# Four edits at the end of the recurrence of a one-layer decoder: row buffer slots, first attention rows, query weights, waits for stores

## The reference, cut to what matters

```python
# x (4, 2048, 512), ctx (4, 77, 512), all float32
x = x + recurrence(layernorm(x), ...)               # diagonal plus low rank state space, over time
x = x + cross_attention(layernorm(x), ctx, Wq, Wk, Wv, Wo)   # 16 heads of 32, 77 keys
x = x + ffn(layernorm(x), ...)                      # expand to 2048, butterflies, gelu, contract
...
def step(z, u_t):                                   # x.reshape(T, B, 8, 64): "T" is the batch axis
    y = A * z + u_t
    z_new = jnp.einsum('hk,bpk->bph', V, y)
    return (z_new, z_new)
```

## Time and profile before

| | us |
|---|---|
| median of 3 runs | 2243.32 (2242.6 to 2244.34) |
| profiled execution, its own time | 2245.92 |
| span of its trace | 2244.1 |
| PE busy | 2208.0 (98%) |
| DVE busy | 1710.0 (76%) |
| ACT busy | 1230.7 (55%) |
| POOL busy | 471.8 (21%) |
| mean granted TensorE clock | 0.992 |

### The profile page before, as it was taken

How to read it: one execution, slowest core, us unless ns; L and a number is a source line. 1 busy time by engine, 2 the same in 40 slices (tenths; PEclk the granted TensorE clock), 3 DMA queues, 4 the chain that set the end, 5 groups by cost and what they waited for, 6 DMA issues and landing times.

```text
span 2244.1 us, 41303 instructions
## 1 busy us (share of the span) xinstructions
PE 2208.0 (98%) x15960; PEld 1938.0 (86%) x15960; DVE 1710.0 (76%) x2868; ACT 1230.7 (55%) x2749; POOL 471.8 (21%) x578
## 2 busy tenths in 40 slices
PE   8999889999999999999999999999999999999999
PEld 7788678888888888789989989989989989889899
DVE  6775588888988888857858858758669578579467
ACT  3666567766666766735536446446346356355343
POOL 3530222232322322200200300300300300201203
PEclk8999899999999999999999999999999999999999
DMA  9999613323323322476785786686676776766765
GB/s 321 338 356 307 211 60 131 119 84 123 126 86 114 123 92 90 168 244 180 217 270 172 223 269 184 214 267 208 198 259 209 226 229 208 250 207 209 227 189 194
DMA packets 202092, 443.36 MB, mean 198 GB/s; under 512 B 32442, under 2 KB 70586, under 8 KB 200362
## 3 DMA queue, kind: packets, MB, share of 16 engines
q1 hardware_dynamic: 201898, 440.72, 60.8%
HBM read 341.66 MB, written 99.01 MB: 196 GB/s over the span
## 4 chain that ended last, share of the span: by engine, by line
PE 88%; DVE 5%; DMA 3%; ACT 2%; issue 1%; SPq 0%; POOL 0%; DVEq 0%; ACTq 0%; POOLq 0%
PE ps L456 71%; PE ps L2027 5%; PE ps L1995 4%; PE ps L2006 3%; DMA x_scratch<-xa 2%; PE ps L1911 1%; PE ps L1954 1%; PE ps L1842 1%; ACT es L1106 1%; DVE st L1299 1%; DMA x<-x_scratch 1%; DVE ptl L1336 1%; PE ps L1884 0%; PE ps L1871 0%; PE ps L1807 0%
## 5 line engine op out<-in xcount | busy, mean ns | idle before, releaser
L456 PE MATMUL ps<-ring,gh 128*128 128x256 f32 x3584 | 652.8, 284 | 0.1
L456 PEld LDWEIGHTS ps<-ring,gh 128*128 128x128 f32 x3584 | 558.2, 192 | 2.2 <-DVE gl L1336 1.5
L456 PE MATMUL ps<-xth,ring 128*128 128x512 f32 x1792 | 553.4, 389 | 0.6 <-ACT U L1216 0.6
L456 PE MATMUL ps<-ring,gl 128*128 128x256 f32 x1792 | 506.8, 283 | 0.0
L456 PEld LDWEIGHTS ps<-xth,ring 128*128 128x128 f32 x1792 | 336.4, 188 | 70.7 <-issue 1.0
L1204 ACT ACTIVATE gh<-G 128x512 fp32r<-128x512 f32 x384 | 239.2, 629 | 218.8 <-PE ps L456 218.2
L456 PE MATMUL ps<-xtl,ring 128*128 128x512 f32 x896 | 348.6, 389 | 0.0
L456 PEld LDWEIGHTS ps<-ring,gl 128*128 128x128 f32 x1792 | 343.5, 192 | 0.0
L1336 DVE TENSOR_TENSOR gl<-G,gh 128x512 fp32r<-128x512 f32 x384 | 276.7, 733 | 51.2 <-ACT gh L1204 50.2
L1187 ACT ACTIVATE G<-G,up_b 128x512 f32<-128x512 f32 x192 | 138.9, 723 | 222.0 <-DVE G L1642 222.0
L1642 DVE TENSOR_TENSOR U<-ps,U 128x512 f32<-128x512 f32 (+1 forms) x167 | 136.1, 815 | 162.8 <-PE ps L456 160.1
(11 more groups left out here) (236 smaller groups left out, 4385.8 us busy)
## 6 DMA issues: line engine op xcount, KB each, us to landing
ring<-wup_scratch SPq DMA_DIRECT2D x224, 512.0 KB, 3.7
ring<-wdn_scratch SPq DMA_DIRECT2D x224, 512.0 KB, 3.6
X<-x_scratch SPq DMA_DIRECT2D x32, 1024.0 KB, 8.8
xa<-in_x SPq DMA_DIRECT2D x16, 1024.0 KB, 8.7
x_scratch<-xa SPq DMA_DIRECT2D x16, 1024.0 KB, 10.7
x<-x_scratch SPq DMA_DIRECT2D x16, 1024.0 KB, 5.6
x_scratch<-x SPq DMA_DIRECT2D x16, 1024.0 KB, 4.3
out_x<-X SPq DMA_DIRECT2D x15, 1024.0 KB, 6.3
```

Of the source, the lines that this page charges most:

```text
L456: mm = pe.matmul(bank, a, b, start=first and i == 0, stop=last and i == n - 1, skip_group_check=go_on)
```

## The change

1. `xslot`: the five row buffers are used in the order 3, 0, 4, 1, 2 instead of 3, 4, 0, 1, 2. So buffer 0 is last used by group 11 (before: 12), buffer 4 by group 12 (before: 11); 1, 2 and 3 by 13, 14 and 15, as before.
2. SP: x1[0] is loaded in group 12 after the wait for the store of group 11 (before: in group 13 after that of group 12). x1[1] is loaded after the store of group 14 has been issued (before: in group 14 ahead of the pieces of c = 2 and 3).
3. ACT makes `wqh` in group 15, c = 0, ahead of the copies of pieces 67 and 68, after the store of group 12 (before: group 14, c = 1, store of group 11). DVE makes `wql` in group 15 after the first add (before: after group 14, ahead of the statistics of x1[0]).
4. SP: in groups 13 to 15 the wait for the store of group g - 1 stands just ahead of the store of group g, behind all the pieces of the group (before: behind the pieces of c = 1).

```diff
-        xslot = lambda g: (g + 3) % XS
+        xslot = lambda g: (3, 0, 4, 1, 2)[g % XS]
...
                     if c == 1:
-                        if g:
+                        if 0 < g <= NG - 4:
                             stored(sp, x1_stored, g - 1)
                         if g and g + 4 < NG:
                             load_x(g + 4)
-                        n = g - (NG - 3)
-                        if n in (0, 1):
-                            after(sp, x1_loaded, n * 16)
-                            sp.dma_start(x1[:, n, :, :], x1_ld[n]).then_inc(x1_loaded, 16)
+                        if g == NG - 4:
+                            sp.dma_start(x1[:, 0, :, :], x1_ld[0]).then_inc(x1_loaded, 16)
+                if g > NG - 4:
+                    stored(sp, x1_stored, g - 1)
                 sp.wait_ge(x1_ready, KC * g + KC)
                 sp.dma_start(x1_st[g], xa[:, xslot(g), :, :]).then_inc(x1_stored, 16)
+                if g == NG - 2:
+                    load_x1(1)
...
-                    if g == NG - 2 and c == 1:
+                    if g == NG - 1 and c == 0:
                         act.wait_ge(wq_loaded, 16)
-                        act.wait_ge(x1_stored, 16 * (NG - 4))
+                        act.wait_ge(x1_stored, 16 * (NG - 3))
                         A(wqh[:, :, :], wq_raw[:, :, :], ACT.Copy, scale=SCALE).then_inc(wq_hi, 1)
...
+                    if g == NG - 1 and c == 0:
+                        dve.wait_ge(wq_hi, 1)
+                        V.scalar_tensor_tensor(wql[:, :, :], wq_raw[:, :, :], SCALE, raw(wqh[:, :, :]), ALU.mult, ALU.subtract).then_inc(wq_lo, 1)
                 if g == NG - 2:
-                    dve.wait_ge(wq_hi, 1)
-                    V.scalar_tensor_tensor(wql[:, :, :], wq_raw[:, :, :], SCALE, raw(wqh[:, :, :]), ALU.mult, ALU.subtract).then_inc(wq_lo, 1)
                     spread2(0, range(T))
                     moments2(0)
```

## The result

| | before | after |
|---|---|---|
| median of the runs | 2243.81 (2239.49 to 2247.56, 18 runs) | 2248.51 (2243.94 to 2251.85, 18 runs) |
| profiled execution, its own time | 2245.92 | 2243.94 |
| span of its trace | 2244.1 | 2242.2 |

The ratio is 1.0021 [1.0014, 1.0027]: +4.7 us. A second series of the changed kernel gave 1.0013 [1.0003, 1.0023]. The profiled execution of after happens to be its fastest, and that of before one of its slower ones, so the two spans stand the wrong way round. Two single traces can't be subtracted here; they have to be compared by stretches.

The account below looks back on a forecast made before the run. The chain into the first scores at 254.6 us was taken as the bound. A 2.9 us later start plus 1.0 us of clock gave +3.9 us, 2243.3 to 2247.2, range 2240.5 to 2251.0.

Parts of the forecast that it names:

- part 2b: x1[1] loaded behind the store of group 14: two pieces and a store go first, 5.7 to 7.7 us; decides the forecast.
- The wait: Before the first scores: x1[1] lands at 247.4, scores follow at 257.5 instead of 254.6, 2.9 us later.
- Frame: Outside the moved stretch: times between 0 and 200 us and after 300 us should not differ in length.
- Turns in the queue: DMA queue: a 1 MB load costs those behind it 2.7 us, a `wd` store 1.35, a group's store 3.0 to 5.0.
- part 2a: x1[0] loaded a group sooner, landing at about 212: `apply2(0)` starts 3.6 us sooner, queries end 1 to 4 sooner, taken 2.
- Parts 1, 3, 4: Slot order, query weights and waits for stores at group ends: each costed at nothing; bounds of 1.9 and 2.3 us for weights.
- head start: Sooner start of the queue work ahead of x1[1], credited from the earlier x1[0] alone: 0 to 2.0 us.
- The slack: Before, x1[1] allowed scores at 251.8 while the queries allowed 254.6: 2.8 us of cover.
- Clock: PE idles 6 us before the first scores, then may run at half speed: 0 to 2 us, taken 1.0.
- Under cover: Rival: x1[1] still lands before 244.5, so the queries set the scores; 2243, between -1.5 and +1; chance 0.18.
- Overtaking: Rival: x1[1] lands ahead of the store, at 242.4, and the earlier x1[0] counts in full; 2238.3; chance 0.11.
- SP late: Rival: SP issues group 14's store late, at 237.7; x1[1] lands at 249.9, scores at 260.0; 2250.7; chance 0.15.

Follow-up runs that it names:

- c_both: Changed kernel with x1[1] loaded ahead of the store of group 14 and `apply2(1)` behind the last `woh` on ACT; 2241.19 us, 0.9990 of before.
- a_x10_back: Changed kernel with x1[0] loaded in group 13 again, after the wait for the store of group 12; 2248.24 us, 1.0014 of before.
- b_x11_last: Kernel before with only x1[1] moved behind the store of group 14; 2248.87 us, 1.0015 of before.
- a_x11_first: Changed kernel with x1[1] loaded just ahead of the store of group 14; 2244.86 us, 0.9999 of before.
- a_waits_back: Changed kernel with the waits for the stores of groups 12 to 14 back behind the pieces of c = 1; 2247.45 us, 1.0010 of before.
- a_weights_back: Changed kernel with `wqh` made in group 14, c = 1, and `wql` after group 14 again; 2248.81 us, 1.0020 of before.
- layout run: Changed kernel with each 256 KB store of pieces 56 to 71 going to one block of 128 rows; 2238.18 us, 0.9970 of before.

## Why the prediction was right, and where it was not

**Forecast.** +3.9 us on the median, 2247.2; the runs gave +4.7 (2248.5) and +4.0. The mechanism was the forecast one, shown by two runs: part 2b alone costs 3.7 us, and without it the change costs nothing that can be told. But the sizes of its terms were wrong. The wait was taken at 2.9 us and comes to 1.1, the clock at 1.0 and comes to 1.4, and about 2 us of the measured loss are in no term at all. That the sum came so near is in part luck.

**Frame.** Right as far as two traces of each kernel tell: no stretch outside T0 to V differs between them beyond its own spread.

**Turns in the queue.** Not borne out for part 2a's followers. The store of group 12, the last `yd` and `ubs` should land 2.7 us later; they land within 0.4 us of before (means of two traces each, counted from T0: 11.3 before and 11.6 after, 17.5 and 17.1, 19.5 and 19.1). But the trace of the kernel that differs from after in this load alone has them 2 to 3 us sooner. Over all runs with the old layout and no fill, `ubs` lands 17.0 to 19.8 after T0 in the four traces with x1[0] late and 17.9 to 19.5 in the six with it early. So whether the load costs those behind it 2.7 us or nothing stays open; the spread of single traces is as large. x1[0] itself takes 8.2 us, fewer than the 9.5 to 11.7 of its neighbours.

**Part 2a.** `apply2(0)` should start 3.6 us sooner; counted from T0 it starts 4.5 sooner (25.0 and 24.5, before 29.5 and 28.9). The copy of piece 69 is done 1.1 us before it (in after), and its last release comes from POOL. The queries end 44.5 and 44.8 after T0, before 50.3 and 48.3: 4.7 sooner in the mean, and not 2. That error had no effect on the sum, since by the forecast the queries don't set the scores. It did hide how much was on the table: c_both takes it.

**Parts 1, 3, 4.** Costed at nothing; taking 3 or 4 back gives no gain that can be told. Part 1 was not tried alone, but a_x10_back has the new slot order with x1[0] late and b_x11_last the old one, and their ratios are 1.0014 and 1.0015.

**Part 2b, landing.** This term was mis-sized. By the letter the first trace, with x1[1] at 243.1, even met the prediction's sign of being wrong in its main term ("lands before 244.5"); the second has 247.8. T0 alone differs by 4.4 us between these two, so a mark in absolute time could not decide it. Counted from T0, x1[1] was taken 5.7 later, with 3.7 as the least; measured are 3.0 (42.1 less 39.1). The turn of the store was right: it costs x1[1] 3.7 us (after against a_x11_first), inside 3.0 to 5.0. The head start was wrong. I credited 0 to 2.0 us, from part 2a only; the store of group 14 is issued 29.8 after T0 (mean of two) instead of 33.4, 3.5 us sooner. And b_x11_last, where x1[0] is as late as before, issues it at 30.4 as well, so most of this head start need not be a gift of part 2a. About half of b_x11_last's 3.0 us come from x1[1] being gone from ahead of pieces 65 and 66: from the landing of group 13's store to the issue of group 14's it takes 1.9 us instead of 3.3. The other half is group 13's store landing sooner in its trace, which its edit doesn't touch. 6.7 (the middle of 5.7 to 7.7) less 3.5 is 3.2.

**Part 2b, from landing to scores.** 10.1 us forecast; 10.0 measured in both traces of after (from 243.1 to 253.14, and from 247.8 to 257.74).

**The slack.** 2.8 us were taken from the one trace of before. In its second trace the scores come 49.96 after T0 and x1[1] lands at the same 39.0: the slack is 0.9. The trace at hand was at the late end in this stretch. So less delay (3.0, not 5.7) met less slack (0.9 to 2.8): +0.2 to +2.1 us, in the mean +1.1, where the sum had +2.9. Against the very trace that the sum was made on, S has not moved at all (51.92 in the first trace of after and 51.96); only the other traces show that it is late.

**Clock.** 1.0 us taken, 0 to 2 bounded, 1.25 measured in the first scores. "No row shows this stretch slow" was settled by after's windows.

**The account.** +1.1 and +1.4 make 2.5 of the 4.7 us by two traces each. Taking in the four other kernels with x1[1] behind the store, the old layout and no fill (b_x11_last, a_x10_back, a_waits_back, a_weights_back), the means are S - T0 51.87 and V - S 44.80: 2.3 over before. The rest, about 2 us, is not located; b_x11_last's own trace holds 3.6 of its 3.7. It may be the spread of single traces (T0 alone varies by 4.4 us), and that stays open.

**The rivals.** Under cover: nearer than its 0.18 says. Its bound, 244.5, is 41.8 after T0, and x1[1] landed 41.9 and 42.2 after T0, just beyond it. It falls by the chain, which starts at this landing, by PE's idle of 7 us, and by b_x11_last, which costs 3.7 us; in executions of before whose queries end as in the second trace, the cover ends at 39.96. Overtaking: fell, in every trace of this order x1[1] lands 3.3 us or more behind the store. Its "less of the stretch at half clock" was an estimate: from 228 to 240 us the mean granted clock is 0.50 and 0.57 in the two traces of before and 0.86 in both of after. SP late: fell; SP was sooner, not later.

## What to carry to other kernels

A load that moves sooner is worth only what its last companion allows: before crediting it, list what else the first consumer needs, with its landing and its own chain, and credit the smaller head start. Take slack from several traces, for a slack of 2.8 us in one trace was 0.9 in the next. Count landings from a mark that every trace has: 243.1 and 247.8 in absolute time were 41.9 and 42.2 after T0. And where the DMA share is low while landings are long (0.73 and 0.76, and 8.3 to 11.6 us for 1 MB, in after), look at the shapes of the transfers before their order: with the new layout the changed kernel stands 7.1 us below before, with the best order tried here 2.9, and the interval of that one holds no change.

## What the runs showed of the hardware

- With the target of the pieces' 256 KB stores changed from 8 x 16 x 512 with the 8 slowest (after) to 128 rows in one block (layout run), the DMA share from 212 to 226 us went from 0.73 to 0.97, and from 226 to 240 us from 0.76 to 1.05 (it adds up the packets' own times). The 1 MB stores of groups 13 and 14 in the same queue landed in 5.3 and 6.6 us instead of 8.3 and 8.8, and the last five stores of pieces 0.59 to 0.64 us apart instead of 1.28 to 1.30. A store to the first target updated its semaphore 9 times, one to the second 16 times.
- Right behind the issue of `ubs` (2048 elements of 4 bytes, 8 KB) SP's next issue took 6.25 us for a 1 MB load (before), and two pieces took 9.26 and 7.67 us (after, layout run). With `ubs` moved, three pieces took 4.90 us in the old place and five took 10.61 behind the new one; the two other blocks of five in after took 6.13 and 6.41.
- Filling an idle stretch of PE with 30 products took the granted clock from 0.50 at 250 to 258 us (after) to 1.00 at 254 to 262 and 0.57 at 262 to 270 us, and bought nothing that can be told (1.0019 against 1.0013 to 1.0021).
